# Spreading a head's softmax reciprocals behind the slot's value products in TensorE's order

## The chip, the cores and the metric

The kernel runs on one core of one Trainium2 chip. The metric is the device time of one execution in microseconds (us). A core has five engines with an instruction queue each, all in order: TensorE (PE), VectorE (DVE), ScalarE (ACT), GpSimd (POOL) and SyncE (SP), which here only issues transfers. Engines wait for each other by semaphores.

## The reference

A decoder layer on x of 4 x 256 x 512, in float32: causal self-attention with rotary positions (32 heads of 16), cross attention over a context of 4 x 1601 x 512, and a feed-forward layer of a dense product and two chosen low-rank experts of 28, each added to x and layer-normalized. The change stands in the cross attention, 32 query heads of 128 that share 8 key and value heads:

```
q = (query @ Wq + bq).reshape(B, L, NKV, G, HDIM)
k_, v_ = jnp.split(kv @ Wkv + bkv, 2, axis=-1)
k = k_.reshape(B, Lk, NKV, HDIM)
v = v_.reshape(B, Lk, NKV, HDIM)
scores = jnp.einsum('blkgd,bmkd->bkglm', q, k) * scale
attn = jax.nn.softmax(scores, axis=-1)
o = jnp.einsum('bkglm,bmkd->blkgd', attn, v).reshape(B, L, NHEAD * HDIM)
return o @ Wo + bo
```

## The kernel before

The four batches run one after the other, each in three stages: self-attention, cross attention, feed-forward. Factors are split in a high and a low half, and each product is made of three matmuls (high by high, high by low, low by high).

The cross attention of a batch takes 32 heads. Scores are held with the keys over the partitions and the 256 queries along the row, so 1601 keys make 13 tiles of 128, the last of 65 rows. Two tiles make a slot: seven slots a head, the seventh with the single short tile. A loop `for g in SLOTS` on every engine goes through the slots of all heads, and a table of offsets says which step of which head an engine does in slot g. With a head's first value products at its slot 0, its scores are made 13 slots ahead (`SCORE`), the exponentials 3 and their low halves 2 slots ahead (`EXP`, `LOW`), so several heads are in work at once. `JOBS` is a table of projections that are laid into the slots: one query job per head (at each head's slot 0, for a later head), key jobs, value jobs (13 in and behind every eighth head, so that three slots in a batch hold a value job and a query job together) and output jobs. Jobs write to a ring of two PSUM banks; a job waits for `freed`, which VectorE raises when the low half of the job two before (`job_low`, L890) has been taken.

A head's softmax goes like this. TensorE makes the scores (`scores`, L1195), ScalarE copies them out (L721, L719), VectorE keeps the maximum over tiles (`maximum`, L931, L928 for the short tile) and folds the two halves of the row (L934). TensorE turns the folded maxima (`turn_maxima`, L1221), VectorE reduces them to one column (`row_maxima`, L941), and TensorE spreads them over the partitions again (`spread_maxima`, L1229). GpSimd subtracts them from the scores (L534). ScalarE makes the exponentials (L739, L744), VectorE their low halves (`low_and_sum`, L952) and sums (L956, L960), TensorE the value products (`weigh`, L1286) into the bank `dn`. For the division, GpSimd folds the sums (L542), TensorE adds them over the partitions (`sum_rows`, in the head's slot 6), VectorE takes the reciprocals `rs` as a column (`row_reciprocals`, L967), TensorE spreads them over the partitions with two transposes against the identity (`spread_reciprocals`, L1308, offset `SUM_ROW` = 7), ScalarE copies the head's sum out of `dn` (`take_heads_sum`, L754), and VectorE multiplies the two (`normalize`, L974, offset `HEAD_SUM` = 7). GpSimd adds the bias and splits the result (`finish_head`, L553 to L557, offset `HEAD_END` = 9) for the output jobs.

In slot g VectorE does, in this order: the low halves of the jobs of slot g - 1; the low half and sum of the exponentials; a head's column maxima; a head's reciprocals; a head's normalization; the maxima of the slot's scores. TensorE's order is written out in the loop at L1316. Its products nearly all go through one helper and carry its line, L1061. In the first batch GpSimd also splits the weights (L524, L526) in three slots of a head. The matmuls of `weigh` of the next head's slot 0 wait for ScalarE's copy of the sum, since they start over in `dn`.

What the spread waits for and what it raises:

```
pe.wait_ge(rs_ok, n + 1)
for tb in range(TB):
    last = nc.tensor.transpose(mbank[:, S + tb * P:S + (tb + 1) * P], rs[:, tb:tb + 1].broadcast_to([P, P]), ident)
last.then_inc(rd_mm, 1)
```

and what stands on VectorE for it:

```
dve.wait_ge(oc_ok, n + 1)
dve.wait_ge(rd_mm, n + 1)
nc.vector.tensor_tensor(orw[:, n % 2, :], mbank[:, S:2 * S], orw[:, n % 2, :], ALU.mult).then_inc(nm_ok, 1)
```

Of the kernel before, what the change touches and what calls it, by code (L numbers as in the profile page):

```python
# [75 lines left out]
MAX_TURN, MAX_COL, MAX_ROW, SUM_FOLD, SUM_COL, SUM_ROW, HEAD_SUM, HEAD_END = -6, -5, -4, 5, 6, 7, 7, 9  # L76
# [3 lines left out]
def slot_of(g, start):  # L80

    h, s = divmod(g - start, NSL)
    return [(h, s)] if 0 <= h < NHB else []


def head_of(g, start):

    h, s = divmod(g - start, NSL)
    return [h] if s == 0 and 0 <= h < NHB else []
# [95 lines left out]
def build(nc, x, x_t, ctx_t, ws, wso, wk_in, wv_in, wq_in, wo_in, bo_s, bo_x, wb, wga, wlb, rope, consts, wk2, wv2, wq2, wo2, out, nb=B):  # L185
    with ExitStack() as ctx:
# [126 lines left out]
        def ring(b, *job_):  # L313
            return b * NJ + JOB_AT[job_]
# [739 lines left out]
        def _(pe):  # L1054
# [5 lines left out]
            def mm(dst, lhs, rhs, first, final):  # L1060
                return nc.tensor.matmul(dst, lhs, rhs, start=first, stop=final)  # L1061
# [8 lines left out]
            for b in range(nb):  # L1070
# [124 lines left out]
                def scores(h, s):  # L1195

                    n = b * NHB + h
                    p = h // NHD
                    k = n * NSL + s
                    if k >= 2:  # L1200
                        a, z = divmod(k - 2, NSL)
                        pe.wait_ge(cp_ok, k - 1)
                        pe.wait_ge(mx_ok, a * NSL + z - (1 if a and z == 0 else 0))
                    pe.wait_ge(freed, ring(b, "Q", p, h % NHD) + RING + 1)
                    if h % G == 0:
                        pe.wait_ge(freed, ring(b, "K", p, h % NHD // G * len(KCH) + chunk_of(s)) + RING + 1)
                    for e, (i, w) in enumerate(KEYS[s]):
                        dst, keys = sbank[k % 2][0:w, e * S:(e + 1) * S], slice(i * P, i * P + w)
                        mm(dst, kh[:, keys], qh[:, h % QH, :], True, False)
                        mm(dst, kh[:, keys], ql[:, h % QH, :], False, False)  # L1210
                        last = mm(dst, kl[:, keys], qh[:, h % QH, :], False, True)
                    last.then_inc(sc_mm, 1)

                def turn_maxima(h):

                    n = b * NHB + h
                    pe.wait_ge(mx_ok, (n + 1) * NSL)
                    if n >= 2:
                        pe.wait_ge(nm_ok, n - 1)
                    for tb in range(TB):  # L1220
                        last = nc.tensor.transpose(mbank[:, tb * P:(tb + 1) * P], mxa[:, tb * P:(tb + 1) * P], ident)  # L1221
                    last.then_inc(tm_mm, 1)

                def spread_maxima(h):

                    n = b * NHB + h
                    pe.wait_ge(mc_ok, n + 1)
                    for tb in range(TB):
                        last = nc.tensor.transpose(mbank[:, tb * P:(tb + 1) * P], mcol[:, tb:tb + 1].broadcast_to([P, P]), ident)  # L1229
                    last.then_inc(mr_mm, 1)  # L1230

                def sum_rows(h):

                    n = b * NHB + h
                    pe.wait_ge(sf_ok, n + 1)
                    pe.wait_ge(mr_ok, n + (2 if h + 1 < NHB else 1))
                    for tb in range(TB):
                        last = mm(mbank[:, tb:tb + 1], suc[:, tb * P:(tb + 1) * P], cst[:, C_ONE:C_ONE + 1], True, True)
                    last.then_inc(sx_mm, 1)
# [46 lines left out]
                def weigh(h, s):  # L1286

                    n, kv = b * NHB + h, h % NHD // G
                    k = n * NSL + s
                    if s == 0:  # L1290
                        pe.wait_ge(oc_ok, n)
                    pe.wait_ge(pl_ok, k + 1)
                    if h % NHD == 0:
                        pe.wait_ge(freed, ring(b, "V", h // NHD, KEYS[s][-1][0]) + RING + 1)
                    dst, w = dn[:, 0:S], slice(kv * P, (kv + 1) * P)
                    for e, (i, r) in enumerate(KEYS[s]):
                        cols = slice(e * S, (e + 1) * S)
                        mm(dst, vh[0:r, i, w], ph[0:r, k % PH, cols], i == 0, False)
                        mm(dst, vh[0:r, i, w], pl[0:r, k % PH, cols], False, False)
                        last = mm(dst, vl[0:r, i, w], ph[0:r, k % PH, cols], False, i == KT - 1)  # L1300
                    last.then_inc(pv_mm, 1)

                def spread_reciprocals(h):

                    n = b * NHB + h
# [4 lines that stand above are left out]
# [6 lines left out]
                for g in SLOTS:  # L1316
                    for h, s in slot_of(g, SCORE):
                        scores(h, s)
                    for h in head_of(g, MAX_ROW):
                        spread_maxima(h)  # L1320
                    for h in head_of(g, SUM_ROW):
                        spread_reciprocals(h)
                    for j in JOBS[g]:
                        run_job(*j)
                    for h in head_of(g, SUM_COL):
                        sum_rows(h)
                    for h, s in slot_of(g, VALUE):
                        weigh(h, s)
                    for h in head_of(g, MAX_TURN):
                        turn_maxima(h)  # L1330
                for j in LAST_JOBS:
# [98 lines left out]
```

## Time and profile before

| | |
|---|---|
| time, median of 3 runs | 2927.25 us (2918.7 to 2929.63) |
| profiled execution, own time | 2911.91 us |
| its span | 2910.1 us |
| TensorE busy | 2707.1 us, 93% |
| VectorE busy | 2076.5 us, 71% |
| ScalarE busy | 1956.8 us, 67% |
| GpSimd busy | 1654.4 us, 57% |
| mean granted TensorE clock | 0.977 |

The busy times are those of one profiled execution, on the core's own clock from its first to its last instruction. A wait in the profile is the idle time of an engine just before an instruction, put down to the instruction that released it. The granted clock is the share of TensorE's full 2.4 GHz that it was given; half of it is 1.2 GHz. Matmuls overlap: the next starts some 0.12 us after the one before while each is shown as 0.28 us long. The cross attention of the four batches reaches from about 130 to 740, 860 to 1450, 1570 to 2160 and 2280 to 2870 us.

### The profile page before, as it was taken

To read this page: it belongs to the slowest core of one execution; us is meant where nothing else is said; L and a number is where in the kernel's file an instruction comes from. 1 tells how busy PE (TensorE), PEld (TensorE's weight loads), DVE (VectorE), ACT (ScalarE), POOL (GpSimd) and SP (SyncE) were. 2 spreads that over 40 slices of the span, in tenths; PEclk is the share of its full clock that TensorE was granted. 3 is DMA by queue.
4 is the path that set the end of the run, shared out by engine and by line. 5 is a ranking of instruction groups with operands and counts; after the bars stand their busy time and mean duration, and the time that the engine had idled before them with its cause. 6 is when DMAs were issued, how large, how long until landed. Compare 5 with 4: busy or idle time off the path is not lost.

```text
span 2910.1 us, 60485 instructions
## 1 busy us (share of the span) xinstructions
PE 2707.1 (93%) x20528; PEld 2495.1 (86%) x20528; DVE 2076.5 (71%) x4140; ACT 1956.8 (67%) x4168; POOL 1654.4 (57%) x1678
## 2 busy tenths in 40 slices
PE   6889999999889999999889999999988999999996
PEld 4688989898569999999757999999976899999995
DVE  3478787878447878787844877777865587878785
ACT  3477676767457777676745877777756577777674
POOL 3279898966215656565711656656552275656563
PEclk8899999999999999999999999999989999999998
DMA  5446565622421212121231122212133121212112
GB/s 170 151 145 218 179 207 181 212 72 73 149 64 38 102 45 102 44 102 45 102 130 47 56 77 66 81 59 88 58 135 95 43 88 44 101 46 92 55 55 102
DMA packets 97919, 285.10 MB, mean 98 GB/s; under 512 B 9936, under 2 KB 18256, under 8 KB 94416
## 3 DMA queue, kind: packets, MB, share of 16 engines
q1 hardware_dynamic: 97616, 281.24, 28.3%
q8 instruction: 169, 2.77, 0.4%
q14 instruction: 134, 1.10, 0.1%
HBM read 237.16 MB, written 44.04 MB: 97 GB/s over the span
## 4 chain that ended last, share of the span: by engine, by line
PE 59%; ACT 5%; issue 5%; DVE 4%; POOL 3%; DMA 1%; DVEq 0%; ACTq 0%; POOLq 0%; SPq 0%
PE bank L1061 34%; PE dn L1061 12%; PE sp L1061 9%; ACT ph L739 2%; POOL kept_s L534 2%; PE bank L1127 1%; ACT sp L744 1%; PE sp L1229 1%; DVE sua L960 1%; PE sp L1308 1%; DVE mcol L941 1%; POOL orw L553 1%; ACT kept_s L721 0%; POOL ol L557 0%; PE sp L1221 0%
## 5 line engine op out<-in xcount | busy, mean ns | idle before, releaser
L534 POOL TENSOR_TENSOR kept_s<-kept_s,mrow 128x512 f32<-128x512 f32 (+1 forms) x896 | 1065.4, 1219 | 574.7 <-ACT mrow L729 574.5
L952 DVE TENSOR_TENSOR pl<-sp,ph 128x512 fp32r<-128x512 f32 (+1 forms) x896 | 576.5, 643 | 61.0 <-ACT sp L744 59.3
L739 ACT ACTIVATE ph<-kept_s 128x512 fp32r<-128x512 f32 (+1 forms) x896 | 534.1, 596 | 46.9 <-POOL kept_s L534 42.2
L744 ACT ACTIVATE sp<-kept_s 128x512 f32<-128x512 f32 (+1 forms) x896 | 506.1, 565 | 4.2 <-DVE sua L960 4.2
L1061 PE MATMUL dn<-ph,vh 128*128 128x256 f32 (+1 forms) x1664 | 491.3, 295 | 2.2 <-DVE pl L952 1.8
L1061 PE MATMUL dn<-ph,vl 128*128 128x256 f32 (+1 forms) x1664 | 472.9, 284 | 0.0
L1061 PE MATMUL dn<-pl,vh 128*128 128x256 f32 (+1 forms) x1664 | 472.4, 284 | 0.0
L960 DVE TENSOR_TENSOR sua<-sp,sua 128x512 f32<-128x512 f32 (+1 forms) x640 | 399.8, 625 | 0.0
L721 ACT ACTIVATE kept_s<-bank 128x512 f32<-128x512 f32 x384 | 228.5, 595 | 225.5 <-PE bank L1061 223.8
L721 ACT ACTIVATE kept_s<-sp 128x512 f32<-128x512 f32 x384 | 228.6, 595 | 182.9 <-PE sp L1061 178.7
L1061 PEld LDWEIGHTS dn<-ph,vh 128*128 128x128 f32 (+1 forms) x1664 | 318.7, 192 | 10.2 <-DVE pl L952 3.4
L1061 PEld LDWEIGHTS dn<-pl,vh 128*128 128x128 f32 (+1 forms) x1664 | 318.0, 191 | 4.1
L1061 PEld LDWEIGHTS dn<-ph,vl 128*128 128x128 f32 (+1 forms) x1664 | 318.0, 191 | 0.0
L1061 PE MATMUL bank<-wvx,ctxh 128*128 128x256 f32 (+1 forms) x1664 | 306.4, 283 | 2.5 <-DVE vl L913 2.0
L1061 PE MATMUL bank<-ctxh,wk 128*128 128x400 f32 (+1 forms) x1024 | 290.4, 346 | 3.2 <-DVE xres L888 3.2
L1061 PEld LDWEIGHTS bank<-wvx,ctxh 128*128 128x128 f32 (+1 forms) x1664 | 251.3, 184 | 6.3 <-DVE vl L913 6.3
L1061 PE MATMUL bank<-qh,kh 128*128 128x256 f32 (+1 forms) x832 | 242.5, 291 | 5.2 <-DVE ql L909 5.2
L553 POOL TENSOR_SCALAR orw<-orw,cst 128x256 f32<-128x256 f32 x128 | 121.7, 951 | 216.4 <-DVE orw L974 216.4
L1061 PE MATMUL sp<-qh,kh 128*128 128x256 f32 (+1 forms) x832 | 238.1, 286 | 0.0
L1061 PE MATMUL bank<-wvx,ctxl 128*128 128x256 f32 (+1 forms) x832 | 234.0, 281 | 0.0
L1061 PE MATMUL bank<-qh,kl 128*128 128x256 f32 (+1 forms) x832 | 233.0, 280 | 0.0
L1061 PE MATMUL bank<-ql,kh 128*128 128x256 f32 (+1 forms) x832 | 233.0, 280 | 0.0
(145 smaller groups left out, 6658.3 us busy)
## 6 DMA issues: line engine op xcount, KB each, us to landing
wqx<-wq SPq DMA_DIRECT2D x128, 512.0 KB, 3.4
wox<-wo SPq DMA_DIRECT2D x64, 1024.0 KB, 4.9
wk<-wk SPq DMA_DIRECT2D x32, 512.0 KB, 3.3
wvx<-wv SPq DMA_DIRECT2D x16, 1024.0 KB, 6.6
raw<-in_ctx_t SPq DMA_DIRECT2D x48, 200.0 KB, 2.5
wqk<-in_ws SPq DMA_DIRECT2D x17, 513.0 KB, 4.0
raw<-in_wq_in SPq DMA_DIRECT2D x32, 256.0 KB, 4.0
wq<-hib SPq DMA_DIRECT2D x32, 256.0 KB, 2.0
```

The source lines that it names most:

```text
L534: nc.gpsimd.tensor_tensor(kept_s[:, n % 2, i:z, :], kept_s[:, n % 2, i:z, :], mrow[:, n % 2, :].unsqueeze(1).broadcast_to([P, z - i, S]), ...
L553: nc.gpsimd.tensor_scalar(o, o, bias, None, ALU.add).then_inc(oh_ok, 1)
L721: nc.scalar.activation(dst, src[:, :], ACT.Copy).then_inc(cp_ok, 1)
L739: nc.scalar.activation(ph[:, k % PH, 0:cols], src, ACT.Exp, scale=XSCALE).then_inc(ph_ok, 1)
L744: nc.scalar.activation(pbank[k % 2][:, 0:cols], src, ACT.Exp, scale=XSCALE).then_inc(pr_ok, 1)
L941: nc.vector.tensor_reduce(mcol[:, :], mbank[:, 0:S].rearrange("p (a n) -> p a n", a=TB), AX.X, ALU.max).then_inc(mc_ok, 1)
L952: nc.vector.tensor_tensor(pl[:, k % PH, 0:cols], src, ph[:, k % PH, 0:cols], ALU.subtract).then_inc(pl_ok, 1)
L960: nc.vector.tensor_tensor(sua[:, 0:cols], src, sua[:, 0:cols], ALU.add).then_inc(su_ok, 1)
L1061: return nc.tensor.matmul(dst, lhs, rhs, start=first, stop=final)
L1127: last = nc.tensor.transpose(s_turn[:, z:z + P], pn[:, n % PNR, a:a + P], ident)
L1229: last = nc.tensor.transpose(mbank[:, tb * P:(tb + 1) * P], mcol[:, tb:tb + 1].broadcast_to([P, P]), ident)
L1308: last = nc.tensor.transpose(mbank[:, S + tb * P:S + (tb + 1) * P], rs[:, tb:tb + 1].broadcast_to([P, P]), ident)
```

## The change

In TensorE's loop over the slots, the two transposes that spread a head's reciprocals are issued behind the slot's jobs and value products in place of ahead of the jobs. Their slot, what they compute, what they wait for and what they raise are the same, and the other engines' orders are the same.

```diff
@@ -1318,14 +1318,14 @@
                         scores(h, s)
                     for h in head_of(g, MAX_ROW):
                         spread_maxima(h)
-                    for h in head_of(g, SUM_ROW):
-                        spread_reciprocals(h)
                     for j in JOBS[g]:
                         run_job(*j)
                     for h in head_of(g, SUM_COL):
                         sum_rows(h)
                     for h, s in slot_of(g, VALUE):
                         weigh(h, s)
+                    for h in head_of(g, SUM_ROW):
+                        spread_reciprocals(h)
                     for h in head_of(g, MAX_TURN):
                         turn_maxima(h)
                 for j in LAST_JOBS:
```

TensorE before, at an ordinary head: the end of the slot's scores (the short tile, into a bank), the spread (`sp<-cst,rs`) and the start of the query job (`bank<-xh,wqx`):

```order
L1061 MATMUL bank<-qh,kh 65x256 [waits freed,mx_ok,cp_ok]
L1061 MATMUL bank<-ql,kh 65x256
L1061 MATMUL bank<-qh,kl 65x256
L1308 MATMUL sp<-cst,rs 128x128 [waits rs_ok]
L1308 MATMUL sp<-cst,rs 128x128
L1061 MATMUL bank<-xh,wqx 128x256 [waits wq_ld0,freed]
L1061 MATMUL bank<-xl,wqx 128x256
```

TensorE now, the end of the same kind of slot: the next head's first value products (`dn<-`), the spread, and the next slot's scores:

```order
L1061 MATMUL dn<-ph,vh 128x256
L1061 MATMUL dn<-pl,vh 128x256
L1061 MATMUL dn<-ph,vl 128x256
L1308 MATMUL sp<-cst,rs 128x128 [waits rs_ok]
L1308 MATMUL sp<-cst,rs 128x128
L1061 MATMUL sp<-qh,kh 128x256 [waits freed,mx_ok,cp_ok]
L1061 MATMUL sp<-ql,kh 128x256
```

The spread has moved past the query job's twelve matmuls and the six value products. At the three slots of a batch with a value job (`bank<-wvx`) and a query job it has moved past both; before, the spread stood ahead of the first of the value jobs:

```order
L1061 MATMUL sp<-qh,kl 65x256
L1308 MATMUL sp<-cst,rs 128x128 [waits rs_ok]
L1308 MATMUL sp<-cst,rs 128x128
L1061 MATMUL bank<-wvx,ctxh 128x256 [waits freed]
L1061 MATMUL bank<-wvx,ctxh 128x256
```

Now it stands one slot's scores ahead of the second value job:

```order
L1308 MATMUL sp<-cst,rs 128x128 [waits rs_ok]
L1308 MATMUL sp<-cst,rs 128x128
L1061 MATMUL bank<-qh,kh 128x256 [waits freed,mx_ok,cp_ok]
L1061 MATMUL bank<-ql,kh 128x256
L1061 MATMUL bank<-qh,kl 128x256
L1061 MATMUL bank<-qh,kh 128x256
L1061 MATMUL bank<-ql,kh 128x256
L1061 MATMUL bank<-qh,kl 128x256
L1061 MATMUL bank<-wvx,ctxh 128x256 [waits freed]
```

VectorE's order is unchanged; around the normalization it reads:

```order
L952 TENSOR_TENSOR pl<-sp,ph 128x512 [waits pv_mm,ph_ok,pr_ok]
L960 TENSOR_TENSOR sua<-sp,sua 128x512 [waits su_ok]
L974 TENSOR_TENSOR orw<-sp,orw 128x256 [waits rd_mm,oc_ok]
L928 TENSOR_TENSOR mxa<-bank,mxa 65x256 [waits mx_ok,cp_ok]
L934 TENSOR_TENSOR mxa<-mxa 128x256 [waits mx_ok]
L909 SCALAR_TENSOR_TENSOR ql<-bank,cst,qh 128x256 [waits job_hi]
```

The instruction that waits for the spread (`rd_mm`) stands ahead of the last maxima and the query job's low half, as before.

## Rows read from the trace of the kernel before

**Rows 1.** The page, busy time by engine.

```profile
PE 2707.1 (93%) x20528; PEld 2495.1 (86%) x20528; DVE 2076.5 (71%) x4140; ACT 1956.8 (67%) x4168; POOL 1654.4 (57%) x1678
```

**Rows 2.** Waits, whole span: who <- for whom: us in total, times, longest.

```profile
POOL orw L553 <- DVE orw L974: 216.4, 86, 5.7
...
PE sp L1308 <- DVE rs L967: 28.4, 36, 1.1
PE sp L1229 <- DVE mcol L941: 24.2, 60, 1.6
```

**Rows 3.** Waits of TensorE in the third batch, 1470 to 2180 us.

```profile
PE sp L1308 <- DVE rs L967: 8.2, 10, 1.1
PE sp L1229 <- DVE mcol L941: 5.4, 15, 1.1
```

**Rows 4.** TensorE in time: start us, us, what, [idle before <- releaser]; 1.1 us waits.

```profile
1090.28 0.43 PE L1308 MATMUL sp<-cst,rs 128*128 128x128 f32 x2 [1.09 <-DVE rs L967]
...
1094.21 0.28 PE L1061 MATMUL sp<-qh,kh 128*128 128x256 f32 x1
...
1384.55 0.43 PE L1308 MATMUL sp<-cst,rs 128*128 128x128 f32 x2 [1.09 <-DVE rs L967]
...
1388.35 0.38 PE L1221 MATMUL sp<-cst,mxa 128*128 128x128 f32 x2
...
1427.79 0.43 PE L1308 MATMUL sp<-cst,rs 128*128 128x128 f32 x2 [1.04 <-DVE rs L967]
```

**Rows 5.** VectorE in time, the fold behind the wait at 1090.28.

```profile
1092.70 0.81 DVE L934 TENSOR_TENSOR mxa<-mxa 128x256 f32<-128x256 f32 x1
```

**Rows 6.** Busy by stretch; behind the POOL figure the granted clock, DMA share, GB/s.

```profile
1088.00:1094.00 6.00, 4.91 (x28) 4.54 (x28) 5.39 (x11) 4.50 (x10) 6.00 (x6) 0.72 0.00 0
```

**Rows 7.** TensorE in time at an ordinary head.

```profile
1122.20 0.38 PE L1308 MATMUL sp<-cst,rs 128*128 128x128 f32 x2
...
1124.56 0.28 PE L1061 MATMUL sp<-qh,kh 128*128 128x256 f32 x1
...
1125.97 0.38 PE L1221 MATMUL sp<-cst,mxa 128*128 128x128 f32 x2
...
1128.77 0.43 PE L1229 MATMUL sp<-cst,mcol 128*128 128x128 f32 x2 [0.30 <-DVE mcol L941]
```

**Rows 8.** VectorE in time at the same head.

```profile
1124.07 0.41 DVE L974 TENSOR_TENSOR orw<-sp,orw 128x256 f32<-128x256 f32 x1
...
1124.85 0.49 DVE L934 TENSOR_TENSOR mxa<-mxa 128x256 f32<-128x256 f32 x1
...
1127.09 0.69 DVE L952 TENSOR_TENSOR pl<-sp,ph 128x512 fp32r<-128x512 f32 x1 [0.17 <-ACT sp L744]
...
1128.30 0.41 DVE L941 TENSOR_REDUCE mcol<-sp 128x2 f32<-128x256 f32 x1
```

**Rows 9.** TensorE in time at a slot with a value and a query job.

```profile
1181.42 0.51 PE L1061 MATMUL bank<-wvx,ctxh 128*128 128x256 f32 x2 [0.16 <-DVE vl L913]
...
1185.09 0.28 PE L1061 MATMUL bank<-qh,kh 128*128 128x256 f32 x1
...
1185.78 0.41 PE L1061 MATMUL bank<-wvx,ctxh 128*128 128x256 f32 x2
```

**Rows 10.** VectorE in time at the same slot.

```profile
1182.81 0.41 DVE L974 TENSOR_TENSOR orw<-sp,orw 128x256 f32<-128x256 f32 x1
...
1183.99 0.41 DVE L913 TENSOR_TENSOR vl<-bank,vh 128x256 fp32r<-128x256 f32 x1
```

**Rows 11.** TensorE in time at a 0.5 us wait, and the turn that follows.

```profile
1053.68 0.43 PE L1308 MATMUL sp<-cst,rs 128*128 128x128 f32 x2 [0.51 <-DVE rs L967]
...
1058.88 0.38 PE L1221 MATMUL sp<-cst,mxa 128*128 128x128 f32 x2
```

**Rows 12.** The fold on VectorE and GpSimd's subtraction beside it, first batch.

```profile
409.13 1.53 DVE L934 TENSOR_TENSOR mxa<-mxa 128x256 f32<-128x256 f32 x1
...
409.10 1.28 POOL L526 TENSOR_TENSOR lob<-raw,hib 128x512 fp32r<-128x512 f32 x1
```

## The prediction

> **What bounds the kernel now.** I read the page first, then the waits of TensorE, then both engines in order of time around the moved step, at four kinds of heads. TensorE is busy for 2707.1 us of the span of 2910.1 us [rows 1], so it is the bound, and time is to be had only where it stands still. The step that moves is itself its largest wait in the attention over the context: 28.4 us in 36 waits on the reciprocals of L967, ahead of 24.2 us on the column maxima of L941 [rows 2]. Each of the batches 2 to 4 holds ten of these waits, worth 8.2 us, and fifteen on the maxima, worth 5.4 us [rows 3]; batch 1 holds the other six. The rest of the argument is what VectorE does then, since it both makes the reciprocals and reads their spread, and its in-order queue holds the fold of the maxima (L934) and the low halves behind that.
>
> Read in order of time, the 36 waits are of three sizes: twenty of 1.0 to 1.1 us (three stand in [rows 4]), twelve of 0.5 us [rows 11] and four of 0.2 us. At the other 92 heads the reciprocals are ready first.
>
> **What moves.** Two transposes per head (128 pairs, the same instructions) go behind the slot's jobs and value products. Nothing is added or taken away, on any engine. The pair holds TensorE for 0.22 us wherever it stands (0.14 us to the next start and 0.08 us by which the start after that is late). Nothing else on TensorE depends on it; on VectorE the normalization (L974) waits for it, and behind that stand the last two maxima, the fold, the low half of the slot's query or value job, and the next slot's low halves. GpSimd's three operations on the finished head start after L974; they feed an output projection at least three slots later and I cost them at nothing: GpSimd already idles 216.4 us ahead of them [rows 2]. The loads of SyncE follow the query job, which comes 0.22 us sooner, and cost nothing either.
>
> **Price of the later normalization.** At an ordinary head the scores after the slot start at 1124.56, so the pair would start 0.22 us ahead of that, at 1124.34. It takes 0.38 us [rows 7], and 0.05 us pass until the reader starts (L941 ends at 1128.71, TensorE starts at 1128.77 [rows 7, 8]). The normalization starts at about 1124.77 in place of 1124.07, 0.70 us later [rows 8]. The fold then ends at 1126.04 in place of 1125.34, and the turning of the maxima (L1221), now at 1125.97 without a wait, comes at about 1126.09: 0.1 us lost. On VectorE there is only 0.17 us of idle up to L941 [rows 8], so the column maxima are up to 0.53 us late, at a place where TensorE already waits 0.30 us [rows 7]. The loss per such head lies between 0.1 and 0.5 us. I take 0.33, in the middle, because ScalarE sits between these steps too and its own lateness is only partly added. Two heads in eight are of this kind in batches 2 to 4: 24 x 0.33 = 8 us. Where an output job (1.4 us) stands ahead of the turn, the delay is covered; without that cover such a head would cost the same 0.1 to 0.5 us.
>
> **Price at a slot with a value job.** Three times a batch the slot holds a value job and a query job, and the next slot opens with another value job that needs the ring bank back. Here the pair moves behind both jobs and the products, to where the next scores start now, 1185.09 [rows 9]. The pair starts there (the value job at 1181.42 waits for VectorE either way, so it comes no sooner), the normalization at 1185.52, and the low half that frees the bank comes 1.18 us behind it (1183.99 less 1182.81 [rows 10]), at 1186.70, ends at 1187.11, and the job starts at 1187.17 in place of 1185.78. That is 1.39 us: 0.22 us is the pair itself and 1.17 us a wait, of which a profile would count about 1.0 us, since the last matmul's end lies 0.16 us behind the point where another could start. Twelve times: 12 x 1.39 = 16.7 us. This is the largest cost and a new wait.
>
> **What the old waits give back.** A 0.5 us wait has an output job ahead of the next turn, which comes 5.20 us after the pair without a wait, so it is kept: 12 x 0.51 = 6.1 us gained [rows 11]. A 1.1 us wait is there because VectorE is late. With the pair later, TensorE runs on, and meets the same late VectorE at the fold: that ends at 1092.70 + 0.81 = 1093.51 [rows 5] whatever TensorE does. In a head of this kind at full clock the turn comes 3.80 us after the pair (1388.35 less 1384.55 [rows 4]); counted from 1090.28 that is 1094.08. It can now come at 1093.56: 0.52 us gained, and 0.3 us of it goes again at L941, whose chain has not moved. I take 0.2 us for 13 of the twenty, 0.6 us for the three at the start of a batch, nothing for the four in a batch's last heads, where the copy of the head's sum on ScalarE comes late instead: 13 x 0.2 + 3 x 0.6 = 4.4 us. So of 28.4 us of waits about 10.5 come back. The waits of batch 1 behind GpSimd stay: there the fold takes 1.53 us beside a subtraction of 1.28 us that GpSimd began 0.03 us earlier [rows 12], so a fold that starts 0.5 us later ends at the same time. The Trainium skill (SBUF — State Buffer, Who interferes with whom) says that the second of two such operations is blocked until the first is done; the trace agrees for this subtraction, and by that rule the sum for batch 1 is nothing as well, where a fold of fixed length would add 0.1 us per head.
>
> **The clock.** The wait of 1.09 us at 1090.28 is followed by matmuls at half speed: from the pair to the scores 3.93 us pass [rows 4] against 2.36 us at the ordinary head [rows 7], with a mean granted clock of 0.72 over six microseconds [rows 6]. That is a fall from 2.4 to 1.2 GHz worth 1.57 us. Seven of the 13 waits of this kind are followed by such a fall. The change breaks the 1.1 us into a wait of some 0.3 us for the head's sum and one of 0.3 to 0.5 us at the turn. No fall in the attention over the context follows waits that short. I take all seven back: 7 x 1.57 = 11 us. The Trainium skill (TensorE: Matmul & The Clock Gate, HAM oscillation — how this bites in real kernels) ties the fall to waits longer than any here; by that rule nothing would come back and the sum would be 11 us higher. The row speaks against it.
>
> **The sum** against the profiled execution (2911.91 us): + 8 + 16.7 - 6.1 - 4.4 - 11 = + 3 us, 2915 us. The median of the runs, 2927.25, lies 15 us above that execution. Ten of the twenty 1.1 us waits show no fall of the clock in it; ten more falls would be 15.7 us, so I read the difference as falls that come or not by chance. Then in a median run the change gives back up to nine falls more, 14 us. Between + 3 and - 11 I take - 3: 2924 us.
>
> **Rivals.**
> (a) The new wait lets the clock fall. TensorE stands still about 1.0 us at the twelve value jobs; the shortest wait that I read a fall behind is 1.04 us [rows 4], so this is at the edge, and my 1.0 carries 0.15 us of doubt. If two in three of them bring a fall, that is 8 x 1.57 = 12.5 us on top: 2937 us, and up to 2943 if all do. This ends slower, and it decides once the wait passes some 1.04 us. For it: the waits of 1.04 and 1.09. Against it: half of the waits even of that size pass without one. Chance 0.22.
> (b) VectorE is behind everywhere, and every head pays its 0.5 us: 128 x 0.5 = 64 less 28: 2963 us. Against it: in batches 2 to 4 VectorE keeps up at the fold, or the turn at 1125.97 would wait [rows 7]. Chance 0.03.
> (c) VectorE is not what holds the turn back, and the whole 28.4 us comes back with the falls: 2927 + 16.7 - 28.4 - 11 = 2904 us. Against it: the fold's end at 1093.51 [rows 5]. It needs the fold to come earlier with nothing that would make it so. Chance 0.07.
> (d) The change does not do what it says: VectorE reaches the normalization late enough at both places, so that the pair costs nothing where it comes ready now and brings nothing where it waits: 2927 us. For it: at a wait of 1.1 us VectorE is late at both. Against it: 1124.07 is before 1124.77. Chance 0.13.
> The forecast has the remaining 0.55.
>
> **How the numbers follow.** A measurement of this kernel can tell a change of 0.5%, 14.6 us, from none: 2912.6 to 2941.9. The forecast's own doubt is that of the 24 heads (0.1 to 0.5 us each, 5 us either way), of the twelve value jobs (0.15 us each, 2 us) and of the falls (7 us either way), so about 9 us either way; a tenth or so of it lies beyond the lower bound. Faster: 0.06 of the forecast and 0.06 of (c). Slower: 0.03 of (b), 0.09 of (a) and 0.02 of the forecast. Same: the rest, 0.74. The range takes in most of the forecast and of (a), and leaves out (b) and most of (c): 2910 to 2943 us.
>
> **What would show it.** In the changed profile: the wait of TensorE for L967 ahead of L1308 gone, from 28.4 to under 1 us; new waits at value jobs for L913, twelve of about 1 us; more at L1221 on L934 and at L1229 on L941, each by several microseconds; a few on the copy of a head's sum at L754; no half-speed matmuls behind L1308 in the middle of a batch. I am wrong if the waits at value jobs are absent or under 0.5 us, if falls of the clock stand behind them (rival a), or if the turn's wait does not grow while that of L967 goes (rival c).

## The result and the profile after

| | before | changed |
|---|---|---|
| median of 12 runs | 2918.3 us (2912.61 to 2929.63) | 2924.9 us (2922.63 to 2930.66) |
| profiled execution, own time | 2911.91 us | 2930.66 us |
| its span | 2910.1 us | 2928.9 us |
| TensorE busy | 2707.1 us | 2714.7 us |

The change is slower: ratio 1.0028, 95% interval 1.0017 to 1.0040, or 6.6 us between the medians. That is within the half per cent that I had given three chances in four, and on the other side of zero from my forecast of 2924 us against 2927.25. The profiled execution of before is faster than all 12 of its timed runs, and that of the change is the slowest of its 12, so the 18.8 us between them must not be read as the effect.

The waits of TensorE over the whole span of the changed kernel (who <- for whom: us in total, times, longest), to be held against [rows 2]:

```profile
POOL orw L553 <- DVE orw L974: 297.1, 86, 7.8
...
DVE rs L967 <- PE sp L1061: 97.7, 73, 2.4
DVE orw L974 <- PE sp L1308: 87.8, 98, 3.0
...
PE sp L1229 <- DVE mcol L941: 35.5, 60, 1.6
...
PE bank L1061 <- DVE vl L913: 17.3, 24, 1.1
...
PE sp L1221 <- DVE mxa L934: 15.7, 37, 1.3
```

The wait of TensorE for the reciprocals ahead of L1308 is gone. In its place VectorE now waits 87.8 us for the spread, a row that the kernel before does not have, and TensorE waits for VectorE behind that: 35.5 us on the column maxima against 24.2, 15.7 us on the fold (L934) against 12.0, and 17.3 us at value jobs against 2.0. The 17.3 us are twelve waits of 1.06 us, at the job that the prediction spoke of, and twelve of 0.38 us at the job ahead of it.

TensorE of the changed kernel in time, at a slot with a value and a query job (start us, us, what, [idle before <- releaser]):

```profile
1047.89 0.38 PE L1308 MATMUL sp<-cst,rs 128*128 128x128 f32 x2
1048.03 0.36 PE L1061 MATMUL bank<-qh,kh 128*128 128x256 f32 x1
...
1048.70 0.28 PE L1061 MATMUL bank<-qh,kl 128*128 128x256 f32 x1
1050.04 0.51 PE L1061 MATMUL bank<-wvx,ctxh 128*128 128x256 f32 x2 [1.06 <-DVE vl L913]
```

and VectorE there:

```profile
1048.38 0.42 DVE L974 TENSOR_TENSOR orw<-sp,orw 128x256 f32<-128x256 f32 x1 [2.67 <-PE sp L1308]
1048.72 0.41 DVE L928 TENSOR_TENSOR mxa<-sp,mxa 65x256 f32<-65x256 f32 x1
1049.16 0.48 DVE L934 TENSOR_TENSOR mxa<-mxa 128x256 f32<-128x256 f32 x1
1049.57 0.41 DVE L913 TENSOR_TENSOR vl<-bank,vh 128x256 fp32r<-128x256 f32 x1
```

The reader should see the order of the two: VectorE stood still for 2.67 us in front of the normalization, and only then did the last maxima, the fold and the low half that gives the ring bank back. None of these three needs the spread. In [rows 9, 10] the value job at this place (1185.78) started without a wait.

The ordinary head of [rows 7, 8] in the changed kernel:

```profile
1133.87 0.38 PE L1308 MATMUL sp<-cst,rs 128*128 128x128 f32 x2
...
1135.68 0.44 PE L1221 MATMUL sp<-cst,mxa 128*128 128x128 f32 x2
...
1138.80 0.43 PE L1229 MATMUL sp<-cst,mcol 128*128 128x128 f32 x2 [0.56 <-DVE mcol L941]
```

```profile
1134.36 0.42 DVE L974 TENSOR_TENSOR orw<-sp,orw 128x256 f32<-128x256 f32 x1 [0.66 <-PE sp L1308]
...
1135.14 0.48 DVE L934 TENSOR_TENSOR mxa<-mxa 128x256 f32<-128x256 f32 x1
...
1138.34 0.41 DVE L941 TENSOR_REDUCE mcol<-sp 128x2 f32<-128x256 f32 x1
```

VectorE waits 0.66 us; the wait for the column maxima is 0.56 us in place of 0.30. And the place of the 1.1 us wait of [rows 4 to 6], which had run at half clock before (the second fence is busy time by stretch, with the granted clock behind the POOL figure):

```profile
1102.46 0.38 PE L1308 MATMUL sp<-cst,rs 128*128 128x128 f32 x2
...
1104.56 0.44 PE L1221 MATMUL sp<-cst,mxa 128*128 128x128 f32 x2 [0.29 <-DVE mxa L934]
...
1107.67 0.43 PE L1229 MATMUL sp<-cst,mcol 128*128 128x128 f32 x2 [0.56 <-DVE mcol L941]
```

```profile
1100.00:1106.00 6.00, 5.59 (x46) 5.19 (x45) 5.96 (x12) 5.23 (x12) 5.85 (x7) 1.00 0.26 89
```

The clock is 1.00 there, where it was 0.72.

**From turning to turning.** Since L1221 comes once a head, the time from one to the next is a ruler that does not depend on what happened earlier. These times are differences of the starts of L1221, in us, for the heads of a period of eight in batches 2 to 4 (the place is that of the turned head within its eight):

| place | before | changed | what lies in it |
|---|---|---|---|
| 1 | 23.46 | 24.99 | the value job that waits |
| 2 | 18.07 | 17.36 | the 0.5 us wait |
| 3 | 21.86 | 22.08 | |
| 4 | 13.35, or 14.9 with a fall of the clock | 12.89 | the 1.1 us wait |
| 5 | 15.18 | 15.52 | the column maxima after it |
| 6 | 15.15 | 15.62 | an ordinary head |
| 7 | 20.99 | 21.30 | an ordinary head, with jobs behind it |
| 0 | 17.53 | 17.48 | |

They repeat within 0.05 us in these batches, except at both ends of a batch: its first place 2 takes 13.9 us before and 13.3 changed, its first place 3 21.0 and 21.3, its last place 6 14.6 and 14.9, and its last place 7 12.9 in both. So the cost and the gain of the change can be read head by head, free of what differs between executions elsewhere.

### The profile page after: what moved, and what is told of

Same layout as the page of the kernel before. It is cut to its first block, busy times and chain, and to the rows that moved or that the text cites. A ratio compares the mean times of both kernels' runs of the same rounds, so it can differ in the third digit from the quotient of the medians.

```text
span 2928.9 us, 60485 instructions
## 1 busy us (share of the span) xinstructions
PE 2714.7 (93%) x20528; PEld 2494.1 (85%) x20528; DVE 2068.5 (71%) x4140; ACT 1951.9 (67%) x4168; POOL 1656.1 (57%) x1678
## 4 chain that ended last, share of the span: by engine, by line
PE 70%; issue 9%; POOL 7%; ACT 6%; DVE 6%; DMA 2%; DVEq 0%; SPq 0%; ACTq 0%; POOLq 0%
PE bank L1061 40%; PE dn L1061 15%; PE sp L1061 11%; POOL kept_s L534 3%; ACT ph L739 2%; DVE sua L960 2%; PE bank L1127 2%; PE sp L1229 1%; DVE pl L952 1%; POOL orw L553 1%; PE sp L1308 1%; POOL lob L526 1%; ACT sp L744 1%; POOL ol L557 1%; POOL hib L524 1%
## 5 line engine op out<-in xcount | busy, mean ns | idle before, releaser
L1061 PEld LDWEIGHTS dn<-ph,vh 128*128 128x128 f32 (+1 forms) x1664 | 316.5, 190 | 24.2 <-ACT orw L754 16.5
L1061 PE MATMUL bank<-wvx,ctxh 128*128 128x256 f32 (+1 forms) x1664 | 307.5, 283 | 17.9 <-DVE vl L913 17.3
L1061 PEld LDWEIGHTS bank<-wvx,ctxh 128*128 128x128 f32 (+1 forms) x1664 | 250.8, 184 | 24.2 <-DVE vl L913 24.2
```

## The experiments

The theory after the result: in the cross attention the change does what the working said, with the value jobs as its largest cost, and that cost is VectorE's queue standing behind the normalization; my adjustment for the median runs was wrong. The rivals: the falls of the clock vary between executions and hide the effect; the loss comes from the pair's new place on TensorE itself; gain and loss cannot be had apart because VectorE is late for both.

### Both kernels profiled again

> The kernel before, unchanged, profiled once more. Theory A (what differs between two executions of this kernel lies in the first stage and between the batches, where TensorE waits for loads and other engines, and not at the 1.1 us waits of the cross attention): the four batches' cross attention, from the first to the last turning of the maxima (L1221), takes 568.5, 546.6, 546.7 and 546.6 us again within 2 us each, and what the span differs by from 2910.1 us lies ahead of and between them. Theory B (my prediction's: falls of the clock come or not by chance at the 1.1 us waits): the cross attention of some batch differs by 1.5 us times a whole number, and the sum of the four by most of what the span differs by.

> The changed kernel, profiled once more. Theory A: the four batches' cross attention takes 568.7, 548.2, 548.5 and 548.4 us again within 2 us each, and a span shorter than 2928.9 us is shorter outside of them (the first turning of the maxima at 153 us rather than 159 us, the distances between the batches 163 us rather than 164 to 166 us). Theory B: falls of the clock in the cross attention differ between the two profiles and make up the difference.

Spans 2916.1 us (own time 2917.88) and 2925.8 us (2927.62). The first and the last L1221 of the third batch, in the order before, before again, changed, changed again:

```profile
1594.15 0.38 PE L1221 MATMUL sp<-cst,mxa 128*128 128x128 f32 x2
...
2140.81 0.69 PE L1221 MATMUL sp<-cst,mxa 128*128 128x128 f32 x2 [0.22 <-DVE mxa L934]
```

```profile
1601.42 0.38 PE L1221 MATMUL sp<-cst,mxa 128*128 128x128 f32 x2
...
2147.92 0.44 PE L1221 MATMUL sp<-cst,mxa 128*128 128x128 f32 x2 [1.06 <-DVE mxa L934]
```

```profile
1607.34 0.38 PE L1221 MATMUL sp<-cst,mxa 128*128 128x128 f32 x2
...
2155.80 0.69 PE L1221 MATMUL sp<-cst,mxa 128*128 128x128 f32 x2 [0.20 <-DVE mxa L934]
```

```profile
1604.43 0.38 PE L1221 MATMUL sp<-cst,mxa 128*128 128x128 f32 x2
...
2152.88 0.69 PE L1221 MATMUL sp<-cst,mxa 128*128 128x128 f32 x2
```

All four batches, and where the rest of a difference lies:

| us | before | before again | changed | changed again |
|---|---|---|---|---|
| up to the first L1221 | 153.0 | 157.0 | 159.1 | 156.6 |
| first to last L1221, sum of four batches | 2208.4 | 2207.1 | 2213.8 | 2213.7 |
| between the batches, sum of three | 489.5 | 491.5 | 495.1 | 495.9 |
| behind the last L1221 | 59.3 | 60.6 | 60.9 | 59.6 |

Theory A holds for the larger part: of the 6.0 us between the two spans of before, 7.3 us lie outside of the cross attention and -1.3 us in it, and the two changed ones agree in it to 0.1 us. Theory B has something to it: of the 13 places with a 1.1 us wait (place 4 of the table, all of batches 2 to 4 and the last of batch 1), 7 took 14.9 us in the first profile of before and 5 in the second, so falls there do come and go. But that is 3 us, not 15, and it was made up for in batch 1. In the changed kernel all 13 take 12.9 us, both times. One difference outside stands in both profiles of the change, and the second expectation missed it: the stretches between the batches are longer by 4 to 6 us in the changed kernel. The profiles have a fall of the clock some 122 us behind a batch's last L1221 in five of its six stretches between batches, and in one of the six of before. The change touches nothing there; it moves the time at which the stage begins. Whether that is more than chance stays open: over the ten other kernels below these stretches take 486 to 498 us, and 490.2 us in one whose TensorE order is that of the change. All that lies outside of the cross attention varies from 698 to 717 us over the 14 profiles.

### Early again at the value jobs, and late only there

```diff
                     for h in head_of(g, MAX_ROW):
                         spread_maxima(h)
+                    for h in head_of(g, SUM_ROW):
+                        if not (h % NHD != NHD - 1):
+                            spread_reciprocals(h)
...
                     for h in head_of(g, SUM_ROW):
-                        spread_reciprocals(h)
+                        if h % NHD != NHD - 1:
+                            spread_reciprocals(h)
```

The edit is against the changed kernel. The second kernel has `==` in place of `!=` in both conditions.

> The changed kernel with the spread at its old place at one head in eight, the ones whose slot holds a value job and a query job (12 heads behind which a value job waits for the ring, 4 last heads of a batch where it moves nothing much). If the later low half of the value job is the largest cost (1.54 us between two turnings in the profile of the change, twelve times, 18.5 us), this runs 18 us faster than the change, about 12 us faster than before: 2906 us, ratio 0.996. If the loss sits in the ordinary heads or in falls of the clock elsewhere, it stays within 5 us of the change: 2920 to 2925 us.

> The kernel before with the spread late at those same heads alone. If each costs 1.54 us and leaves the clock as it is: 18 us slower than before, 2937 us, ratio 1.0063. If the waits of about 1 us at the value jobs let the clock fall too: up to 12 x 1.57 us more, 2955 us, ratio 1.0127, with half-speed matmuls behind them in the trace. If VectorE's lateness is caught up elsewhere: no change.

Early at the value jobs: 2911.6 us, ratio to before 0.9982 (0.9971 to 0.9993), 13.3 us faster than the change. Late only there: 2929.57 us, ratio 1.0041 (1.0028 to 1.0055), 12 us slower than before. Place 1 takes 23.46 us in the first and 24.98 in the second, in all twelve. The waits of TensorE at value jobs, early and late:

```profile
PE bank L1061 <- DVE vl L913: 2.0, 12, 0.2
```

```profile
PE sp L1308 <- DVE rs L967: 28.1, 34, 1.1
...
PE bank L1061 <- DVE vl L913: 17.3, 24, 1.1
```

The largest cost is where it was forecast, and moving it away turns the sign of the change. Both kernels moved by 12 to 13 us where 18 were expected. In the profile of the first the cross attention takes 2197.3 us, 16.5 less than in the change, so most of what is missing lies outside of it. In the second only one of the 13 waits of 1.1 us was followed by a fall, against 7 and 5 before, which gives back some 6 to 9 us that were not expected. Its period of eight heads is 1.5 us longer; that this is the reason is not shown. That the waits of 1.06 us at the value jobs let the clock fall, my rival (a), is refuted: place 1 is 1.53 us longer and not once 3 us, in both profiles of the change and in this kernel.

### Late at two heads in eight

```diff
+                        if not (h % NHD in (0, 2)):
+                            spread_reciprocals(h)
...
+                        if h % NHD in (0, 2):
+                            spread_reciprocals(h)
```

> The kernel before with the spread late only at the heads 0 and 2 of each eight, the ones that wait 0.5 and 1.1 us for the reciprocals in batches 2 to 4. If the gain and the loss of the change sit at different heads: 12 x 0.7 us kept behind the 0.5 us waits, 13 x 0.15 us behind the 1.1 us waits (0.48 at the turn, less 0.33 at the column maxima), and some seven falls of the clock of 1.5 us each, less up to 2.5 us a batch for a fall between two batches: about 15 us faster than before, ratio 0.995 (0.993 to 0.997). If gains and losses cannot be had apart, because VectorE is late for both: within 4 us of before.

2900.74 us, ratio 0.9940 (0.9926 to 0.9955). The 1.1 us heads take 12.89 us, all 13 of them, place 2 takes 17.36 us, place 1 stays at 23.45, and places 6 and 7 stay at 15.15 and 21.00. The expectation held: the gain and the loss sit at different heads and can be had apart.

### Behind the jobs, ahead of the value products

```diff
-                    for h in head_of(g, SUM_ROW):
-                        spread_reciprocals(h)
                     for j in JOBS[g]:
                         run_job(*j)
+                    for h in head_of(g, SUM_ROW):
+                        spread_reciprocals(h)
                     for h in head_of(g, SUM_COL):
```

> The spread behind the slot's jobs but ahead of its value products, 0.71 us earlier than in the change. At an ordinary head the pair then starts at 1123.63 of the trace of before and the normalization could start at 1124.06, where it starts anyway (1124.07): no loss there. At a value job the delay is 0.7 us less: 12 x 0.7 to 0.8 us in place of 12 x 1.54. The gain at the 0.5 and 1.1 us waits stays. If this working holds: 8 to 16 us faster than before, ratio 0.995 to 0.997, and 15 to 20 us faster than the change. If the place behind the jobs is what costs, no better than the change.

2906.8 us, ratio 0.9967 (0.9955 to 0.9980). Place 6 takes 15.10 us and place 7 20.98, as before, and place 1 takes 24.28, so 0.83 us are lost at a value job in place of 1.53: the 0.71 us by which the pair stands earlier are what the normalization and all behind it are sooner. The working of the delay holds at this third point too.

### The normalization one slot later in VectorE's order

```diff
-                    for h in head_of(g, HEAD_SUM):
+                    for h in head_of(g, HEAD_SUM + 1):
                         normalize(h)
```

> The changed kernel with the normalization (L974) one slot later in VectorE's order, behind the low halves of the slot's jobs and ahead of the next slot's maxima, so that nothing on VectorE waits for the spread. If the loss of the change is VectorE's queue standing behind the normalization: the waits at value jobs fall from 17.3 us to 2 us or less, the ones for the column maxima from 34 to 25 us, and the kernel is 25 us faster than the change, about 18 us faster than before: ratio 0.994. If the loss comes from the pair's place on TensorE itself (or the waits for ScalarE's copy), it stays within 5 us of the change.

> The kernel before with the same move of the normalization alone, the control of the run above. The spread is ready at the normalization there, so VectorE waits for nothing less: within 4 us of before, with the 28 us of waits for the reciprocals as they were. If the move helps by itself (the fold comes 0.33 us sooner), it is 5 us or more faster.

2924.43 us, ratio 1.0026 (1.0014 to 1.0038), and 2933.42 us, ratio 1.0055 (1.0040 to 1.0071). Both expectations failed; by its time alone the first would speak for the rival, since it lies within 5 us of the change. I had overlooked a wait of TensorE that stands in the code: `turn_maxima` waits for `nm_ok` of two heads earlier, since it writes the bank that the normalization reads. The largest wait of TensorE in the changed kernel with this move, and its wait at value jobs:

```profile
PE sp L1221 <- DVE orw L974: 70.3, 56, 1.9
...
PE bank L1061 <- DVE vl L913: 4.6, 12, 0.4
```

So this edit put a wait of its own in place of the one removed, and its time says nothing about the theory. The control has that wait too (53.0 us in 52), and lost 15 us. Taking the turn's wait away was not tried, since nothing would then order the two engines in that bank.

Place by place the two kernels say more than their times. At place 1 nothing on VectorE waits for the spread any more, and the low half stands ahead of the normalization:

```profile
1033.73 0.42 DVE L913 TENSOR_TENSOR vl<-bank,vh 128x256 fp32r<-128x256 f32 x1
...
1036.80 0.41 DVE L974 TENSOR_TENSOR orw<-sp,orw 128x256 f32<-128x256 f32 x1
```

All twelve waits of 1.06 us are gone (the 4.6 us are the twelve of 0.38), and place 1 takes 23.65 us, against 23.45 in the control, though the pair stands where the change put it. So 1.33 of the 1.53 us lost there were VectorE's queue, and 0.2 us belong to the pair's place on TensorE; at places 4 to 7 the two kernels agree within 0.05 us at nearly every head, and at four of the nine heads of place 3 in batches 2 to 4 the first is 0.1 to 0.2 us longer. The waits for the column maxima fell to 3.5 us, where 25 were expected.

### The normalization behind the slot's maxima

```diff
-                    for h in head_of(g, HEAD_SUM):
-                        normalize(h)
                     for h, s in slot_of(g, SCORE):
                         if s:
                             maximum(h, s)
+                    for h in head_of(g, HEAD_SUM):
+                        normalize(h)
```

> The changed kernel with the normalization behind the slot's last maxima and the fold in VectorE's order, in the same slot. While VectorE waits for the spread it has then done the maxima and the fold (0.33 + 0.45 + 0.40 us), which wait for nothing of it. If the loss of the change is VectorE's queue standing behind the normalization: the low half at a value job is some 0.8 us earlier than in the change (12 x 0.8 us), the ordinary heads lose nothing, and it is 15 to 25 us faster than the change, 8 to 18 us faster than before: ratio 0.994 to 0.997. The turn waits for the normalization too (that is what the next-slot experiment ran into), but that ends at 1125.2 in the times of the trace of before, ahead of the turn at 1125.97. If the pair's place on TensorE is the cost: within 5 us of the change.

> The control: the kernel before with the same move on VectorE alone. The spread is ready there when VectorE comes to it, so nothing is waited for less: the same as before within 5 us, the 28 us of waits for the reciprocals as they were, the turn up to 0.33 us later or sooner. If the order on VectorE helps by itself, most of the gain of the run above appears here too.

On the changed kernel: 2891.41 us, ratio 0.9911 (0.9897 to 0.9924), 33 us faster than the change. On the kernel before: 2914.12 us, ratio 0.9989 (0.9980 to 0.9998). VectorE of the first at a slot with a value job:

```profile
1036.03 0.41 DVE L928 TENSOR_TENSOR mxa<-sp,mxa 65x256 f32<-65x256 f32 x1
1036.47 0.43 DVE L934 TENSOR_TENSOR mxa<-mxa 128x256 f32<-128x256 f32 x1
1038.79 0.42 DVE L974 TENSOR_TENSOR orw<-sp,orw 128x256 f32<-128x256 f32 x1 [1.89 <-PE sp L1308]
1039.13 0.41 DVE L913 TENSOR_TENSOR vl<-bank,vh 128x256 fp32r<-128x256 f32 x1
```

and the waits of that kernel, for the spread, the column maxima and at value jobs:

```profile
DVE orw L974 <- PE sp L1308: 28.1, 17, 2.1
...
PE sp L1229 <- DVE mcol L941: 24.8, 58, 1.5
...
PE bank L1061 <- DVE vl L913: 7.1, 24, 0.4
```

VectorE does the maxima and the fold first, so 28.1 us of waits for the spread are left of 87.8, and the normalization and the low half follow each other directly. Place 1 takes 24.14 us, place 4 12.61, place 6 15.11, place 7 20.99. The pair stands on TensorE exactly where the change put it, and places 6 and 7 take what they took before the change: their loss was VectorE's order. Place 1 keeps 0.69 of its 1.53 us, since the low half there still stands behind the normalization, and so behind the spread; the experiment before this one has it ahead, and there 0.2 us are left.

The 33 us are more than the 15 to 25 expected. In the profiles the cross attention is 30.0 us shorter than in the change. The value jobs give 0.85 us each, as expected; not counted in the expectation was that places 4 and 5, at and behind the old 1.1 us wait, become 0.28 us shorter each. By the ratio of the control the move by itself is worth 0.1%, some 3 us, of the 0.9%.

### The two halves together

The pair behind the jobs, but at its old place where the slot holds a value job; and the same with the normalization behind the maxima.

> The spread behind the slot's jobs, ahead of its value products, and at its old place where the slot holds a value job and a query job. Per eight heads the behind-jobs run showed 0.8 us lost at the value job and 0.1 us or less elsewhere, so against that run this gains 12 x 0.8 = 10 us: 2897 us, ratio 0.993. It combines the two halves of the explanation; if they do not add, it is no better than the behind-jobs run (0.9967).

> The run above and the normalization behind the maxima. Once the spread comes in time for the normalization, little is left to be waited for: within 4 us of the run above, ratio 0.992 to 0.993. If VectorE is still held at the normalization there, 5 us or more faster than it.

2891.37 us, ratio 0.9914 (0.9900 to 0.9928), and 2889.61 us, ratio 0.9899 (0.9884 to 0.9915). The halves add: in the profile of the first, place 1 is back at 23.46 us, and the cross attention is 10.5 us shorter than in the behind-jobs run, for 10 expected. The last kernel is the fastest of the study; it is not told apart from the changed kernel with the normalization behind the maxima. By their medians the two are within 2 us, as expected, but in the profiles the cross attention of the second is 12.6 us shorter and the rest of its span 17.5 us longer, so what the move is worth there stays open.

## Why the prediction was right and wrong

**What bounds the kernel**: right in the main. The gains and losses read from place to place are waits of TensorE for VectorE, and falls of the clock behind such waits. The exception is the pair's own 0.2 us at a value job.

**Price of the later normalization**: the place was right and the count too small. A delay of 0.70 us was forecast; VectorE waits 0.66 us where it idled nothing. Place 6 lost 0.46 us and place 7 lost 0.31, both within the bounds of 0.1 to 0.5 us. But place 3 lost 0.2 us, which I had not counted. Over a batch that is 0.9 (place 7, three times), 1.7 (place 6, four times, once only 0.3) and 0.6 (place 3, three times), some 3.3 us in place of 2.7.

**Price at a value job**: right. 1.53 us were measured for 1.39, and the new wait is 1.06 us for a forecast of about 1.0. Over twelve that is 18.4 us for 16.7. The split of it held as well: 0.22 us were put down to the pair itself and the rest to a wait, and with the wait gone 0.2 us are left.

**What the old waits give back**: right in kind. The 0.5 us waits gave 0.71 rather than 0.51 us (8.5 us for 6.1). For the new wait I had added 0.16 us, by which a profile counts a wait too short; for the old ones I forgot it, and 0.51 and 0.16 make 0.67. The 13 waits of 1.1 us gave 0.46 at the turn and lost 0.33 at the column maxima, forecast 0.52 and 0.3. The three at the start of a batch gave 0.6 as forecast, but the head behind them lost 0.3. Together these sixteen gave some 2.5 us for 4.4. The four in a batch's last heads gave nothing between turnings, as forecast.

**The clock**: right. All falls behind the 1.1 us waits of place 4 are gone, seven of 1.54 us, in both profiles of the change. The rule of the Trainium skill (TensorE: Matmul & The Clock Gate, HAM oscillation — how this bites in real kernels), by which none would come back, did not hold here: seven of 13 waits of 1.1 us were followed by a fall, and with these waits gone, none of 13.

**The sum**: + 3 us against the profiled execution. Measured over the four cross attentions, which is all that the change touches, it is 2213.8 less 2208.4, + 5.4 us; against the second profile of before, + 6.7 us, next to the 6.6 us between the medians of the runs. The sum had the right sign, and its closeness is partly luck: the ordinary heads cost 1.9 us more, the value jobs 1.7 more, the 1.1 us waits gave 1.9 less, and the 0.5 us waits 2.4 more.

**The step that failed** is the one behind it: "so I read the difference as falls that come or not by chance. Then in a median run the change gives back up to nine falls more", by which + 3 became - 3. The 15 us between the profiled execution and a median of three runs were explained by a mechanism that fitted their size. Twelve runs, these three among them, put the median at 2918.3, not 2927.25, and the second profile of before has fewer falls at these waits than the first, five and not seven; what it is longer by lies in the first stage and between the batches. The change has none of these falls, so against the two profiles of before it gives back seven and five, and not up to sixteen; it ran 6.6 us slower where - 3 was forecast. How many falls a run without a profile has is not shown. Left at + 3, the forecast would have been on the right side.

Of the rivals, (a) had its waits, of 1.06 us, but no fall behind any of them; (b) and (c) did not come; and (d), no difference, is outside the interval by a little.

## What to carry to other kernels

When a producer is moved back in one engine's order, look at its consumer's in-order queue first: what stands behind the waiting instruction and does not need it pays the bill. Move the consumer back too, behind that work; here it turned a loss of 0.3% into a gain of 0.9%. Before the consumer is moved further, read who waits for it, also for a buffer or a bank and not for its data.

A difference between one profiled execution and the median of a few runs is no term of a sum until a second profile shows where it lies.

## What the runs showed of the hardware

The same wait does not always let TensorE's clock fall. Waits of 1.1 us for the reciprocals were followed by a fall from 2.4 to 1.2 GHz at 7 of 13 places in one execution of before and 5 of 13 in another, at 6 of 13 in the kernel before with the normalization behind the maxima, and at 1 of 13 in the kernel that was late at value jobs only, though its waits for L967 were nearly the same (28.1 us in 34, for 28.4 in 36). The waits of 1.06 us at the value jobs were followed by none in 36 (two executions of the change, one of the kernel late there only). Each fall cost 1.54 us. With the wait broken in two pieces of 0.3 to 0.6 us, none of 13 places had one, in either execution of the change.

Nor is a longer wait the surer one. In the changed kernel with the normalization one slot later, the turn at these 13 places waits 1.6 us, and no fall stands behind any of them; the first line is one such wait, the second the six microseconds from it, at a clock of 1.00:

```profile
1091.80 0.41 PE L1221 MATMUL sp<-cst,mxa 128*128 128x128 f32 x2 [1.61 <-DVE orw L974]
```

```profile
1091.80:1097.80 6.00, 6.00 (x46) 5.73 (x47) 5.21 (x10) 3.40 (x8) 4.39 (x5) 1.00 0.01 3
```

What decides whether a fall comes is not shown.
